# Last stage of an edge-gated graph layer: the add of the v part moves from GpSimd to VectorE, two tiles ahead, and gates and masks are handed on in halves

## Chip, cores and metric

The kernel runs on one core of a Trainium2 chip. The core has TensorE (PE, matrix products), VectorE (DVE), ScalarE (ACT), GpSimd (POOL) and SyncE (SP, which here only issues DMA), each with its own instruction queue that is worked off in order. On-chip memory is SBUF, with 128 partitions, and PSUM, eight banks into which TensorE writes. Engines wait for each other by semaphores. The metric is the device time of one execution in microseconds, lower is better.

## What is computed

```python
B, C, D = (16, 128, 256)            # x is 16 x 1024 x 256, adj 1024 x 1024
pre_u = einsum('bud,dk->buk', h_t, W1[:d])
pre_v = einsum('bvd,dk->bvk', h_t, W1[d:])
hidden = relu(pre_u[:, :, None, :] + pre_v[:, None, :, :] + b1)
S = sigmoid(einsum('buvk,ko->buvo', hidden, W2)[..., 0] + b2[0])
a_t = einsum('buv,bud->bvd', S * A_a, h_t)
m_t = einsum('uv,bud->bvd', A_m, h_t) * h_t
z_t = beta1 * h_t + beta2 * (einsum('bvd,de->bve', a_t, Wa) + ba) + beta3 * (einsum('bvd,de->bve', m_t, Wm) + bm)
```

Both A_a and A_m are adj, about 6% of whose entries are not zero. Only at those entries is S needed.

## The kernel before

Everything is float32. Earlier stages compute, per node, h_t Wa (`hWa_dram`) and all of z_t that does not depend on S (`base_dram`); then, for the entries (u, v) of adj that are not zero, a number per batch (`sum_dram`, 1024 x 1024 x 16). What is left of the gate's argument is a part of u and a part of v. The last stage, from line 1400 on, puts the gate together, masks it with adj and multiplies.

It goes over 8 v tiles (`vt`) of 128 nodes, and in each over 8 u tiles (`t`), 64 steps `k = 8 vt + t` in all. One step takes these passes over a 128 (u) x 128 (v) x 16 (batch) block of 1 MiB:

- SyncE loads the block into `raw` (2 buffers) in the order u, v, batch, and 64 KiB of adj into `adj_b` (5 buffers). Three larger loads stand in the same queue: `hWa_all`, 2 MiB for each u tile during the first v tile; `of_v`, 1 MiB for each v tile, one buffer, issued when all adds of the v tile before have read it; and `z`, 2 MiB for each v tile, one buffer, at t = 4, when the finished z of the v tile before has been stored.
- The add (L1457): `masked = raw + of_v`, written in the order u, batch, v. `masked` has 4 buffers, and `step_done(k - 4)` waits until TensorE has read the one to be written.
- The gates (L1513): ScalarE, 16 activations, one for each batch, in place, with the u part as bias.
- The mask (L1475): VectorE multiplies the gates by adj, in place.
- The product (L1493): TensorE, for each batch, `masked` (128 x 128) by `hWa_all` (128 x 256), summed over the eight t into one half of a PSUM bank. All eight banks are in use. In the trace a batch shows as 2 MATMUL instructions, a step as 32.
- `finish(vt)` (L1466): VectorE adds the eight banks to `z`, one after the other. It stands at t = 1 of the next v tile. TensorE may write a bank for the next v tile when it has been added. ScalarE issues the store of z (L1505) behind the gates of t = 3.

The names in what follows: "add t=5" is the add of the step t=5 of a v tile, "raw t=5" its load.

Of the kernel before, what the change touches and what calls it, by code (L numbers as in the profile page):

```python
# [5 lines left out]
def gnn_edges_kernel(nc, x, adj, W1, b1, W2, b2, Wa, ba, Wm, bm, beta1, beta2, beta3, out):  # L6
# [15 lines left out]
    ALU = mybir.AluOpType  # L22
# [3 lines left out]
    B, N, D = x.shape  # L26
# [39 lines left out]
    with ctx:  # L66
# [1332 lines left out]
        with ExitStack() as phase:  # L1399
            RAW, GM, ADJ = 2, 4, 5  # L1400
# [29 lines left out]
            with nc.Block() as block:  # L1430
                @block.sync
                def _(sp):
                    for vt in range(NT):
                        for t in range(NT):
                            k = vt * NT + t
                            if t == 0 and vt:
                                sp.wait_ge(raw_added, k)
                                load_of_v(sp, vt)
                            waits(sp, raw_added, k - RAW + 1)
                            sp.dma_start(raw[k % RAW][:], sum_uv[t * P:(t + 1) * P, vt * P:(vt + 1) * P, :]).then_inc(raw_loaded[k % RAW], 16)  # L1440
                            waits(sp, gate_masked, k - ADJ + 1)
                            sp.dma_start(adj_b[k % ADJ][:], adj[t * P:(t + 1) * P, vt * P:(vt + 1) * P]).then_inc(adj_loaded[k % ADJ], 16)
# [5 lines left out]

                @block.gpsimd
                def _(pool):  # L1450
                    for vt in range(NT):
                        pool.wait_ge(of_v_loaded, 16 * (vt + 1))
                        for t in range(NT):
                            k = vt * NT + t
                            pool.wait_ge(raw_loaded[k % RAW], 16 * (k // RAW + 1))
                            step_done(pool, k - GM)
                            nc.gpsimd.tensor_tensor(masked[k % GM][:].rearrange("p b v -> p v b"), raw[k % RAW][:], of_v[:], ALU.add).then_inc(raw_added, 1)  # L1457

                @block.vector
                def _(dve):  # L1460
# [8 lines left out]
                    nc.vector.tensor_scalar(of_u[:], of_u[:], half_sign[:, 0:1], betas[:, 3:4], ALU.mult, ALU.add).then_inc(u_ready, 1)  # L1469
                    for vt in range(NT):  # L1470
                        for t in range(NT):
                            k = vt * NT + t
                            dve.wait_ge(adj_loaded[k % ADJ], 16 * (k // ADJ + 1))
                            dve.wait_ge(gate_made, k + 1)  # L1474
                            nc.vector.tensor_tensor(masked[k % GM][:], masked[k % GM][:],  # L1475
                                                    adj_b[k % ADJ][:].rearrange("p (a v) -> p a v", a=1).broadcast_to([P, B, P]),
                                                    ALU.mult).then_inc(gate_masked, 1)
                            if t == 1 and vt:
                                finish(vt - 1)
                    finish(NT - 1)  # L1480
# [66 lines left out]
```

## Time and profile before

| | us |
|---|---|
| median of 3 runs | 3941.08 (3937.64 to 3946.14) |
| profiled execution | 3951.05, of it span 3949.3 |
| last stage, from 3368 to 3949 | 581 |
| TensorE busy in it | 474.0 |
| ScalarE busy in it | 400.3 |
| GpSimd busy in it | 330.8 |
| VectorE busy in it | 258.8 |

The span is the time from the first to the last instruction or transfer of one profiled execution. Busy time is the sum over the instructions of an engine, without its waits. TensorE's clock is granted in two levels, 1.2 and 2.4 GHz; its mean in the last stage is 0.91 of the full level.

### The profile page before, as it was taken

To read this page: it belongs to the slowest core of one execution; us is meant where nothing else is said; L and a number is where in the kernel's file an instruction comes from. 1 tells how busy PE (TensorE), PEld (TensorE's weight loads), DVE (VectorE), ACT (ScalarE), POOL (GpSimd) and SP (SyncE) were. 2 spreads that over 40 slices of the span, in tenths; PEclk is the share of its full clock that TensorE was granted. 3 is DMA by queue.
4 is the path that set the end of the run, shared out by engine and by line. 5 is a ranking of instruction groups with operands and counts; after the bars stand their busy time and mean duration, and the time that the engine had idled before them with its cause. 6 is when DMAs were issued, how large, how long until landed. Compare 5 with 4: busy or idle time off the path is not lost. (4 is left out here: it accounts for less than half of the span.)

```text
span 3949.3 us, 56078 instructions
## 1 busy us (share of the span) xinstructions
PE 3452.5 (87%) x14232; PEld 2670.5 (68%) x14232; DVE 2832.8 (72%) x4788; ACT 2318.1 (59%) x14050; POOL 1859.7 (47%) x2338
## 2 busy tenths in 40 slices
PE   4977877887877949999999999999999999578898
PEld 2655555555555637887888888888888887567677
DVE  4455555555555358999999999999999999354534
ACT  0111111111111127998999999999999998577765
POOL 2222222212112125666666666666666665465664
PEclk9989988998988979999999999999999999789999
DMA  4545544555465577566765666765766653956564
GB/s 147 187 168 199 208 171 168 184 209 180 175 217 189 194 178 161 140 172 150 170 157 141 150 137 166 169 168 133 185 145 163 158 128 71 316 203 228 185 214 164
DMA packets 342892, 685.83 MB, mean 174 GB/s; under 512 B 38782, under 2 KB 252648, under 8 KB 319720
## 3 DMA queue, kind: packets, MB, share of 16 engines
q1 hardware_dynamic: 304544, 612.07, 53.6%
q0 software_dynamic: 21504, 53.31, 4.4%
q10 hardware_dynamic: 16512, 16.78, 1.3%
q8 instruction: 116, 1.90, 0.2%
q14 instruction: 216, 1.77, 0.2%
HBM read 444.01 MB, written 256.18 MB: 177 GB/s over the span
## 5 line engine op out<-in xcount | busy, mean ns | idle before, releaser
L1169 ACT ACTIVATE junk<-psum_a 128x128 f32<-128x128 f32 x6144 | 1605.3, 296 | 238.3 <-PE psum_a L1073 172.3
L1169 ACT ACTIVATION_READ_ACCUMULATOR junk<-psum_a 128x1 f32 x6144 | 1381.8, 227 | 0.0
L1114 DVE TENSOR_REDUCE group_sum<-psum_d 128x56 f32<-128x896 f32 x1024 | 1111.2, 1085 | 84.7 <-PE psum_d L1073 44.6
L1072 PE MATMUL psum_d<-u_t,pk 128*128 128x512 f32 x2560 | 1006.5, 393 | 62.2 <-DMA v_t<-rows_dram 33.0
L1073 PE MATMUL psum_d<-v_t,pk 128*128 128x512 f32 x2560 | 999.9, 391 | 0.0
L1218 POOL DMA_INDIRECT sum_dram<-total,idx_all x512 | 505.8, 988 | 228.0 <-POOL total L1229 124.1
L1072 PEld LDWEIGHTS psum_d<-u_t,pk 128*128 128x128 f32 x2560 | 482.2, 188 | 186.0 <-issue 50.2
L1072 PE MATMUL psum_a<-u_t,pk 128*128 128x512 f32 x1536 | 605.6, 394 | 0.0
L1073 PE MATMUL psum_a<-v_t,pk 128*128 128x512 f32 x1536 | 599.3, 390 | 0.0
L1493 PE MATMUL z_psum<-hWa_all,masked 128*128 128x256 f32 x2048 | 474.0, 396 | 118.1 <-DVE masked L1475 71.3
L849 POOL TENSOR_TENSOR own<-whole 128x256 f32<-128x256 f32 x128 | 92.4, 722 | 998.6 <-issue 729.4
L1073 PEld LDWEIGHTS psum_d<-v_t,pk 128*128 128x128 f32 x2560 | 482.6, 189 | 98.4
L1493 PEld LDWEIGHTS z_psum<-hWa_all,masked 128*128 128x128 f32 x2048 | 407.2, 200 | 184.9 <-DVE masked L1475 74.5
L603 PE MATMUL wide<-adj_sb,h 128*128 128x512 f32 x1024 | 511.6, 622 | 0.0
L1513 ACT ACTIVATE masked<-masked,of_u,half_sign 128x128 f32<-128x128 f32 x1024 | 399.0, 480 | 151.7 <-POOL masked L1457 151.7
L673 ACT COPY hWa<-ring 128x512 f32<-128x512 f32 x64 | 37.5, 586 | 715.4 <-PE ring L625 715.4
L1475 DVE TENSOR_TENSOR masked<-masked,adj_b 128x2048 f32<-128x2048 f32 x64 | 220.3, 3445 | 307.8 <-ACT masked L1513 307.8
L1457 POOL TENSOR_TENSOR masked<-raw,of_v 128x2048 f32<-128x2048 f32 x64 | 330.9, 5186 | 230.0 <-DMA raw<-sum_dram 169.2
L1211 POOL TENSOR_TENSOR fold<-group_sum,group_sign 128x256 f32<-128x256 f32 x256 | 189.7, 741 | 394.6 <-DVE group_sum L1141 392.8
L587 PE MATMUL ring<-W_k,hT 128*128 128x258 f32 x1024 | 277.6, 431 | 108.9 <-ACT whole L666 107.5
L1111 DVE TENSOR_REDUCE late_sum<-psum_d 128x4 f32<-128x512 f32 x512 | 347.0, 678 | 0.4 <-PE psum_d L1073 0.4
L1072 PEld LDWEIGHTS psum_a<-u_t,pk 128*128 128x128 f32 x1536 | 289.0, 188 | 77.6 <-ACT junk L1169 20.5
(207 smaller groups left out, 4039.7 us busy)
## 6 DMA issues: line engine op xcount, KB each, us to landing
u_t<-rows_dram SPq DMA_DIRECT2D x126, 1024.0 KB
rows_dram<-split SPq DMA_DIRECT2D x128, 512.0 KB, 3.3
sum_dram<-zero SPq DMA_DIRECT2D x128, 512.0 KB, 5.0
pk<-pick_dram SPq DMA_DIRECT2D x512, 128.0 KB, 2.7
raw<-sum_dram SPq DMA_DIRECT2D x64, 1024.0 KB, 7.0
v_t<-rows_dram SPq DMA_DIRECT2D x36, 1024.0 KB, 13.1
whole_dram<-whole SPq DMA_DIRECT2D x128, 256.0 KB, 3.8
pick_dram<-pick SPq DMA_DIRECT2D x128, 256.0 KB, 2.0
```

Of the source, the lines that this page charges most:

```text
L587: last = nc.tensor.matmul(ring[:, w * BANK:w * BANK + CW], hT[:, c, t * P:(t + 1) * P], W1_k[:, c, w, :], start=(c == 0), stop=(c == DT - 1))
L603: last = nc.tensor.matmul(wide[:, c * N + n * BANK:c * N + (n + 1) * BANK], h[b % 2][:, t, c * P:(c + 1) * P], adj_sb[:, t, n * BANK:(n + ...
L1072: nc.tensor.matmul(dst, pk[n % PKS][:, at:at + P], part(u_t[k % 2][:], b, LB), start=True, stop=False)
L1073: return nc.tensor.matmul(dst, pk[n % PKS][:, SLOTS + at:SLOTS + at + P], part(v_t[n % VG][:], b, LB), start=False, stop=True)
L1111: return nc.vector.tensor_reduce(out_, in_, AX, ALU.add, apply_absolute_value=True)
L1114: nc.vector.tensor_reduce(out_[:, :, 1:EG], in_[:, :, GW:LATE].rearrange("p b (g k) -> p b g k", k=GW), AX, ALU.add, apply_absolute_value= ...
L1169: last = nc.scalar.activation(junk[:, a % RING_A, k * LATE:(k + 1) * LATE], psum_a[a % RING_A][:, k * LATE:(k + 1) * LATE], ACT.Abs, accum ...
L1218: nc.gpsimd.indirect_dma_start(out=sum_dram[:, :], out_offset=bass.IndirectOffsetOnAxis(ap=at, axis=0), in_=sums, in_offset=None, bounds_c ...
L1457: nc.gpsimd.tensor_tensor(masked[k % GM][:].rearrange("p b v -> p v b"), raw[k % RAW][:], of_v[:], ALU.add).then_inc(raw_added, 1)
L1475: nc.vector.tensor_tensor(masked[k % GM][:], masked[k % GM][:], adj_b[k % ADJ][:].rearrange("p (a v) -> p a v", a=1).broadcast_to([P, B, P ...
L1493: last = nc.tensor.matmul(z_psum[b // 2][:, (b % 2) * D:(b % 2 + 1) * D], masked[k % GM][:, b, :], hWa_all[:, t, b, :], start=(t == 0 and ...
L1513: last = nc.scalar.activation(masked[k % GM][:, b, :], masked[k % GM][:, b, :], ACT.Sigmoid, bias=of_u[:, t, b:b + 1], scale=half_sign[:, ...
```

## The change

The add goes from GpSimd, which has nothing left to do in this stage, to VectorE, with the same operands and the same output order. In VectorE's queue the adds of the steps 0 and 1 come first, then in each step k the add of step k+2 ahead of the mask of step k. At t = 1 `finish` stands ahead of the add and the mask, where it stood behind the mask. The gates are handed to VectorE after 8 and 16 batches, the mask is done in two instructions of 8 batches, and TensorE waits for each half. SyncE issues `adj_b` ahead of `raw`, no longer behind it.

```diff
-            RAW, GM, ADJ = 2, 4, 5
+            RAW, GM, ADJ, MASKS = 2, 4, 5, 2
...
+                            waits(sp, gate_masked, MASKS * (k - ADJ + 1))
+                            sp.dma_start(adj_b[k % ADJ][:], adj[t * P:(t + 1) * P, vt * P:(vt + 1) * P]).then_inc(adj_loaded[k % ADJ], 16)
                             waits(sp, raw_added, k - RAW + 1)
                             sp.dma_start(raw[k % RAW][:], sum_uv[t * P:(t + 1) * P, vt * P:(vt + 1) * P, :]).then_inc(raw_loaded[k % RAW], 16)
-                            waits(sp, gate_masked, k - ADJ + 1)
-                            sp.dma_start(adj_b[k % ADJ][:], adj[t * P:(t + 1) * P, vt * P:(vt + 1) * P]).then_inc(adj_loaded[k % ADJ], 16)
...
-                @block.gpsimd
-                def _(pool):
-                    for vt in range(NT):
-                        pool.wait_ge(of_v_loaded, 16 * (vt + 1))
-                        for t in range(NT):
-                            k = vt * NT + t
-                            pool.wait_ge(raw_loaded[k % RAW], 16 * (k // RAW + 1))
-                            step_done(pool, k - GM)
-                            nc.gpsimd.tensor_tensor(masked[k % GM][:].rearrange("p b v -> p v b"), raw[k % RAW][:], of_v[:], ALU.add).then_inc(raw_added, 1)
...
+                    def add_of_v(k):
+                        if k % NT == 0:
+                            dve.wait_ge(of_v_loaded, 16 * (k // NT + 1))
+                        dve.wait_ge(raw_loaded[k % RAW], 16 * (k // RAW + 1))
+                        step_done(dve, k - GM)
+                        nc.vector.tensor_tensor(masked[k % GM][:].rearrange("p b v -> p v b"), raw[k % RAW][:], of_v[:], ALU.add).then_inc(raw_added, 1)
+
+                    HB = B // MASKS
+                    for k in range(2):
+                        add_of_v(k)
                     for vt in range(NT):
                         for t in range(NT):
                             k = vt * NT + t
-                            dve.wait_ge(adj_loaded[k % ADJ], 16 * (k // ADJ + 1))
-                            dve.wait_ge(gate_made, k + 1)
-                            nc.vector.tensor_tensor(masked[k % GM][:], masked[k % GM][:],
-                                                    adj_b[k % ADJ][:].rearrange("p (a v) -> p a v", a=1).broadcast_to([P, B, P]),
-                                                    ALU.mult).then_inc(gate_masked, 1)
                             if t == 1 and vt:
                                 finish(vt - 1)
+                            if k + 2 < NT * NT:
+                                add_of_v(k + 2)
+                            dve.wait_ge(adj_loaded[k % ADJ], 16 * (k // ADJ + 1))
+                            for m in range(MASKS):
+                                rows_ = masked[k % GM][:, m * HB:(m + 1) * HB, :]
+                                dve.wait_ge(gate_made, MASKS * k + m + 1)
+                                nc.vector.tensor_tensor(rows_, rows_,
+                                                        adj_b[k % ADJ][:].rearrange("p (a v) -> p a v", a=1).broadcast_to([P, HB, P]),
+                                                        ALU.mult).then_inc(gate_masked, 1)
...
-                            pe.wait_ge(gate_masked, k + 1)
                             for b in range(B):
+                                if b % (B // MASKS) == 0:
+                                    pe.wait_ge(gate_masked, MASKS * k + b * MASKS // B + 1)
...
-                            last.then_inc(gate_made, 1)
+                                if (b + 1) % (B // MASKS) == 0:
+                                    last.then_inc(gate_made, 1)
```

What this does to VectorE's queue is seen at the turn from the first to the second v tile. Before, VectorE's rows from the mask of t=4 of the first v tile to the first add to z are (masked1 and adj_b0 are buffers; the brackets name the semaphores that a row waits for):

```order
L1475 TENSOR_TENSOR masked0<-masked0,adj_b4 128x2048 [waits gate_made,adj_loaded4]
L1475 TENSOR_TENSOR masked1<-masked1,adj_b0 128x2048 [waits gate_made,adj_loaded0]
L1475 TENSOR_TENSOR masked2<-masked2,adj_b1 128x2048 [waits gate_made,adj_loaded1]
L1475 TENSOR_TENSOR masked3<-masked3,adj_b2 128x2048 [waits gate_made,adj_loaded2]
L1475 TENSOR_TENSOR masked0<-masked0,adj_b3 128x2048 [waits gate_made,adj_loaded3]
L1475 TENSOR_TENSOR masked1<-masked1,adj_b4 128x2048 [waits gate_made,adj_loaded4]
L1466 TENSOR_TENSOR z<-z,z_psum0 128x512 [waits z_summed,z_loaded]
```

After the change, from the second half of the mask of t=4 to the mask of t=7, the add into masked0 that waits for of_v being that of t=0 of the second v tile:

```order
L1481 TENSOR_TENSOR masked0<-masked0,adj_b4 128x1024 [waits gate_made]
L1465 TENSOR_TENSOR masked3<-raw1,of_v 128x128x16 [waits gate_used,raw_loaded1]
L1481 TENSOR_TENSOR masked1<-masked1,adj_b0 128x1024 [waits gate_made,adj_loaded0]
L1481 TENSOR_TENSOR masked1<-masked1,adj_b0 128x1024 [waits gate_made]
L1465 TENSOR_TENSOR masked0<-raw0,of_v 128x128x16 [waits gate_used,raw_loaded0,of_v_loaded]
L1481 TENSOR_TENSOR masked2<-masked2,adj_b1 128x1024 [waits gate_made,adj_loaded1]
L1481 TENSOR_TENSOR masked2<-masked2,adj_b1 128x1024 [waits gate_made]
L1465 TENSOR_TENSOR masked1<-raw1,of_v 128x128x16 [waits gate_used,raw_loaded1]
L1481 TENSOR_TENSOR masked3<-masked3,adj_b2 128x1024 [waits gate_made,adj_loaded2]
```

The add that waits for `of_v` and its `raw` now stands ahead of the mask of t=6 (masked2) in the same queue.

SyncE's queue before, from the load of z at t=4 of the second v tile to the first two raw loads of the third (raw0 and raw1 are the two buffers):

```order
L1447 DMA z<-base_dram 128x16x256 [waits z_stored]
L1440 DMA raw1<-sum_dram 128x2048 [waits raw_added]
L1442 DMA adj_b3<-in_adj_dram 128x128 [waits gate_masked]
L1440 DMA raw0<-sum_dram 128x2048 [waits raw_added]
L1442 DMA adj_b4<-in_adj_dram 128x128 [waits gate_masked]
L1440 DMA raw1<-sum_dram 128x2048 [waits raw_added]
L1442 DMA adj_b0<-in_adj_dram 128x128 [waits gate_masked]
L987 DMA of_v<-linear_dram 128x2048 [waits raw_added]
L1440 DMA raw0<-sum_dram 128x2048 [waits raw_added]
L1442 DMA adj_b1<-in_adj_dram 128x128 [waits gate_masked]
```

The same place after the change:

```order
L1447 DMA z<-base_dram 128x16x256 [waits z_stored]
L1440 DMA adj_b3<-in_adj_dram 128x128 [waits gate_masked]
L1442 DMA raw1<-sum_dram 128x2048 [waits raw_added]
L1440 DMA adj_b4<-in_adj_dram 128x128 [waits gate_masked]
L1442 DMA raw0<-sum_dram 128x2048 [waits raw_added]
L1440 DMA adj_b0<-in_adj_dram 128x128 [waits gate_masked]
L1442 DMA raw1<-sum_dram 128x2048 [waits raw_added]
L987 DMA of_v<-linear_dram 128x2048 [waits raw_added]
L1440 DMA adj_b1<-in_adj_dram 128x128 [waits gate_masked]
L1442 DMA raw0<-sum_dram 128x2048 [waits raw_added]
```

Each raw load has moved behind the adjacency load of its step; the loads of z and of_v stand where they stood.

## Rows read from the trace of the kernel before

**Rows 1.** The page's first line.
```profile
span 3949.3 us, 56078 instructions
```

**Rows 2.** The last stage: length, busy us of each engine (instructions), clock, DMA share, GB/s.
```profile
3368.00:3949.00 581.00, 474.00 (x2048) 407.20 (x2048) 258.76 (x128) 400.26 (x1025) 330.84 (x64) 0.91 0.63 220
```

**Rows 3.** Waits of the last stage: who for whom, total us, times, longest us.
```profile
DVE masked L1475 <- ACT masked L1513: 307.8, 55, 14.4
POOL masked L1457 <- DMA raw<-sum_dram: 169.2, 30, 13.1
ACT masked L1513 <- POOL masked L1457: 151.7, 44, 8.6
...
PE z_psum L1493 <- DVE masked L1475: 71.3, 11, 36.2
...
PE z_psum L1493 <- DVE z L1466: 46.8, 7, 15.3
```

**Rows 4.** Timeline of a v tile: start us, us, engine, line, what, count.
```profile
3603.98 4.86 DVE L1466 TENSOR_TENSOR z<-z,z_psum 128x512 f32<-128x512 f32 x8
...
3604.80 36.23 PE L1493 MATMUL z_psum<-hWa_all,masked 128*128 128x256 f32 x160 [3.08 <-DVE z L1466]
3608.51 2.04 ACT L1513 ACTIVATE masked<-masked,of_u,half_sign 128x128 f32<-128x128 f32 x5 [0.29 <-POOL masked L1457]
...
3610.19 0.38 ACTq L1505 DMA_DIRECT2D out_dram<-z  x1
...
3617.72 0.37 SPq L1447 DMA_DIRECT2D z<-base_dram  x1
...
3620.87 0.43 SPq L1442 DMA_DIRECT2D adj_b<-in_adj_dram  x1
...
3628.36 9.06 POOL L1457 TENSOR_TENSOR masked<-raw,of_v 128x2048 f32<-128x2048 f32 x2 [10.25 <-DMA raw<-sum_dram]
...
3642.97 0.32 SPq L987 DMA_DIRECT2D of_v<-linear_dram  x1
...
3645.14 22.67 PE L1493 MATMUL z_psum<-hWa_all,masked 128*128 128x256 f32 x96 [4.11 <-DVE masked L1475]
...
3650.72 24.25 POOL L1457 TENSOR_TENSOR masked<-raw,of_v 128x2048 f32<-128x2048 f32 x4 [7.79 <-DMA raw<-sum_dram]
...
3671.29 36.46 PE L1493 MATMUL z_psum<-hWa_all,masked 128*128 128x256 f32 x160 [3.48 <-DVE z L1466]
```

**Rows 5.** TensorE in stretches of 4 us: busy us (instructions), granted clock, DMA share, GB/s.
```profile
3604.80:3608.80 4.00, 4.00 (x12) 0.63 0.39 152
3608.80:3612.80 4.00, 4.00 (x20) 1.00 0.41 140
```

**Rows 6.** Single lines: duration in ns, least/median/most, first and last start.
```profile
L1457 POOL TENSOR_TENSOR masked<-raw,of_v x64: 4528/4556/6631, 3368.0 to 3911.2; 128x2048 f32<-128x2048 f32 x64
...
L1475 DVE TENSOR_TENSOR masked<-masked,adj_b x64: 2275/2302/5798, 3380.2 to 3924.6; 128x2048 f32<-128x2048 f32 x64
...
L857 POOL TENSOR_TENSOR base<-base,bias_row x16: 4492/4496/6583, 97.3 to 1353.9; 128x2048 f32<-128x2048 f32 x16
...
L809 DVE TENSOR_TENSOR rank<-rank,row_start x8: 1224/1224/1227, 170.1 to 1144.1; 128x1024 f32<-128x1024 f32 x8
...
L777 DVE COPY counts<-rank x8: 176/4282/4294, 99.6 to 1026.3; 128x16 f32<-128x16 f32 x8
...
L815 DVE COPY lcount<-over_scan x8: 153/153/154, 175.7 to 1149.7; 128x1 f32<-128x1 f32 x8
...
L813 DVE TENSOR_SCALAR over<-rank x8: 693/694/696, 172.6 to 1146.7; 128x1024 f32<-128x1024 f32 x8
```

**Rows 7.** Timeline of the first v tile's end.
```profile
3435.01 23.67 PE L1493 MATMUL z_psum<-hWa_all,masked 128*128 128x256 f32 x96 [9.38 <-DVE masked L1475]
...
3436.98 4.55 POOL L1457 TENSOR_TENSOR masked<-raw,of_v 128x2048 f32<-128x2048 f32 x1 [4.26 <-DMA raw<-sum_dram]
```

**Rows 8.** Timeline of the last v tile.
```profile
3917.94 22.67 PE L1493 MATMUL z_psum<-hWa_all,masked 128*128 128x256 f32 x96 [4.05 <-DVE masked L1475]
```

## Prediction

> **What bounds the kernel now.** I read the span first [rows 1], then the stretch in which the changed code runs [rows 2]. It lasts 581 of 3949.3 us, and everything before it is untouched. In it TensorE is busy 474.0 us, ScalarE 400.3, GpSimd 330.8, VectorE 258.8: TensorE leads, but idles 107 us. The waits of the stretch come next [rows 3]: TensorE waits for VectorE's masks (71.3 us) and for its adds to z (46.8 us), VectorE for ScalarE's gates (307.8 us), ScalarE for GpSimd (151.7 us), and GpSimd for the loads of raw (169.2 us). So the chain runs load, add, gate, mask, matmul, and the loads pace it at two places of every v tile. Both are seen in the timeline [rows 4], where t counts the u tiles of a v tile from 0 to 7.
>
> First place, the store. At 3608.51 ScalarE starts the gates of t=3. The store of z is triggered at 3610.19, SyncE may issue the load of z only at 3617.72, when the store has landed, and raw of t=5 stands behind that load: GpSimd can add it at 3628.36. That is 19.85 us from the end of add t=3 (the gates follow it at once) to the start of add t=5. Second place, of_v. SyncE reloads the only of_v buffer at 3642.97, once add t=7 is done, and add t=0 of the next v tile starts at 3650.72: 7.75 us. Today only GpSimd stands still there; VectorE goes on masking tiles that are already gated, so TensorE's two pauses per v tile are short. The period is 3671.29 less 3604.80, 66.5 us.
>
> TensorE's own pace comes from the same rows: 160 instructions in 36.23 us and 96 in 22.67, both begun after a pause, so 64 take 13.56, a u tile (32) takes 6.8 us, and the first one after a pause 22.67 less 2 x 6.8, 9.1 us. The reason is in [rows 5]: in the 4 us from 3604.80, straight after an idle time, the granted clock averages 0.63 of 2.4 GHz (so most of it at 1.2), and 12 instructions show; in the next 4 us it is 1.00 and 20 show.
>
> **The change, part by part.** *Removed:* 64 adds on GpSimd, median 4556 ns [rows 6]. They also slowed the masks: the mask has a minimum of 2275 ns and a maximum of 5798 [rows 6], and VectorE's busy time of 258.8 [rows 2] less the adds to z, 8 x 4.86 [rows 4], is over 3.4 us a mask. That is freed time on an engine that waited 307.8 us anyway, and I book no gain for it by itself.
>
> *Halved masks:* 128x1024 of two SBUF operands takes 1224 ns on VectorE [rows 6], so a tile costs 2.45 us in place of 2.30, and TensorE may begin 1.2 us after the mask starts. Gates in halves cost ScalarE nothing: the same 16 activations, one more semaphore.
>
> *Added to VectorE:* 64 adds whose output steps 512 bytes from element to element (16 batches inside, 128 v outside), inputs contiguous. No row of VectorE shows such a write of this size. Bounds from the nearest rows: below, its contiguous 128x2048 multiply, 2.3 us; above, GpSimd's run of this very add, 4.53 us. GpSimd's rows don't tell whether the step costs anything: its contiguous add of that size takes 4496 ns and the stepping one 4556 [rows 6]. Two small VectorE rows do: the copy of 16 elements that lie 256 bytes apart takes 176 ns, the copy of one element 153, so 23 ns for 15 elements, 1.53 ns each; two-operand contiguous work costs (2302 - 1224)/1024 = 1.05. If stepping costs the add what lies between these two, 0.5, its element takes 1.53 ns and the add 3.2 us. But a contiguous one-operand instruction runs at (694 - 153)/1023 = 0.53 ns [rows 6]; if the copy would have done so too, stepping cost it 1.0, and the add would take 2048 x 2.05, 4.2 us. I take **3.6 us**, between these two, also near the middle of the outer bounds. The Trainium skill (Vector Engine (DVE) Microarchitecture Reference, section 5.2, Measured stream behaviour on trn2) says that a port keeps its full rate only in runs of at least two adjacent words, and lists 1.71 ns per column for an output hopping 4 KiB at each element, 2.50 for steps of 24 words. No row here shows either; by its 1.71 the add would be an estimated 3.58 us and the result below the same within 1 us, by 2.50 an estimated 5.2 us and some 4045 us in all.
>
> *Moved in the queues:* the adjacency load now stands ahead of raw on SyncE. It has long been free to go, but takes 0.43 us of issue [rows 4], so raw t=5 and raw t=0 each come 0.4 us later where they are issued right behind z and of_v.
>
> *The new waits, which decide.* add k+2 stands ahead of mask k in VectorE's queue. A wait of the add for its raw, for of_v or for TensorE to free a buffer (tile k-2 done) now also holds mask k, and with it TensorE. What was GpSimd's wait becomes everybody's.
>
> **One v tile after the change**, followed on VectorE from the end of add t=3, a being the price of an add:
> 1. Gates of t=3, store, load of z, raw t=5: 19.85 + 0.4 = 20.3 us. Only mask 1, add t=4 and mask 2 (8.5 us) lie beside it; VectorE stands 11.8 us.
> 2. add 5, mask 3, add 6, mask 4, add 7: 3a + 4.9. add 7 needs TensorE done with t=3, which starts 1.25 us after the end of add 5 and, after its pause, takes 9.1: 10.35 against 4.9 + a, a wait of 5.45 - a.
> 3. of_v and raw t=0: 7.75 + 0.4, say 8.1. Beside it lies mask 5 alone (2.45).
> 4. add 0, mask 6, add 1, mask 7, the same wait of 5.45 - a for t=6, add 2, mask 0, the 8 adds to z (4.86 us [rows 4]), add 3: 4a + 7.35 + 4.86 + the wait.
>
> Sum: 20.3 + 4.9 + 8.1 + 7.35 + 4.86 = 45.5, with the rest 45.5 + 7a + 2(5.45 - a) = 56.4 + 5a. At 3.6: **74.4 us against 66.5**.
>
> First v tile: loads arrive back to back and set it as before, so add 7 starts at 3437.0 as now [rows 7]. It ends at 3440.6, add 0 of the next tile runs 3448.7 to 3452.3, mask 6 frees TensorE at 3453.55, t=6 takes 9.1 and t=7 6.8: done 3469.45, where today it is 3458.7 [rows 7]. From there to the end of add 3 another 7.7 us (add 2 at 3462.65, mask 0, the adds to z, add 3 to 3477.16).
> Last v tile: no of_v behind it: 7.7 + 20.3 + 3.6 + 1.25 + 9.1 + 4 x 6.8 = 69.15.
> End: TensorE done at 3469.45 + 6 x 74.4 + 69.15 = 3985.0. Today the tail from TensorE's end at 3940.6 [rows 8] to the span's end is 8.7 us and it stays: span 3993.7, 44.4 above 3949.3. The profiled execution took 3951.05 where the runs have a median of 3941.08, so it lies 10 us above them, and I add the difference to the median: **3985.5 us**, 1.1% slower.
>
> **Rivals.**
> A, *the stepping write is free* (2.3 us, the contiguous row). Then TensorE doesn't pause before t=6 and the second wait is 0.85: period 45.5 + 16.1 + 3.15 + 0.85 = 65.6. First tile done 3466.85, last 65.25: 3925.7, span 3934.4, 14.9 less: 3926 us, faster. It decides below an add of about 2.65 us. For it: nothing else on VectorE is slow. Against: the 1.53 ns row. 0.13.
> Between, an add of 2.5 to 2.8 us: within 0.2%. 0.07.
> B, *the write costs as on GpSimd or more* (4.53): waits 0.92, period 79.05, first tile done 3471.3, last 72.0: 4017.6, span 4026.3, 77 more: 4018 us. 0.07.
> C, *two tiles ahead hides the loads*, and TensorE is the bound: 8 x 6.8 + 2.3 = 56.7 a period, 7 x 9.8 = 69 less: 3872 us. Against it: raw has two buffers, and [rows 4] show raw t=5 held by the store, not by an add. 0.03.
> My forecast, adds of 2.8 to 4.4 us, has 0.70.
>
> **Numbers.** About 0.2% (8 us) is what a measurement of this kernel can tell from no change. Within the forecast the prices 3.2 and 4.2 give about 3967 and 4007 (A and B lie 46 us an us of add below it and 35 above); the store and load times may be off by 1 us each in 7 periods. The upper end takes in B at 4018. Downwards I go to 3938, which holds the in-between case and leaves out A and C, 0.16. Faster: A, C and a third of the between, 0.18; same 0.05; slower 0.77.
>
> **What the changed profile would show.** The add on VectorE near 3.6 us (below 2.65 the sign turns); masks of 1.22 us with hardly any spread; two VectorE waits per v tile for raw, some 12 and 5.5 us, in place of GpSimd's; TensorE idle some 10 us before t=3 and 3 before t=6, with the lower clock after each; period near 74 us; no TensorE pause at a v tile's start beyond the first add to z. Wrong it is if TensorE runs on through t=3 (then the gates or the store come earlier than I think), or if raw t=5 is added sooner than 20 us after add t=3.

## The result, and the profile after

The changed kernel takes 3993.81 us (median of 4 runs, 3988.0 to 3995.45), the kernel before 3939.36 on the same chip (4 runs, 3934.83 to 3946.14): a ratio of 1.0134, interval 1.0116 to 1.0153. It is slower by 1.3%, some 54 us. The range of the prediction (3938 to 4018) holds the time, which lies 8.3 us above the 3985.5 forecast. The profiled span is 3991.4 us, where [rows 1] had 3949.3 and the forecast said 3993.7. The stage itself grew by more than the 42.1 us between the spans: its first VectorE instruction (L1459, L1469 before) starts at 3362.79 us where it started at 3365.52, since the unchanged stages ahead of it happened to end 2.7 us sooner. From there to the end of the span it is 628.6 us in place of 583.8, 44.8 more.

First the last stage as a whole, as in [rows 2] but in a window that begins 8 us sooner, and under it the costliest group of TensorE and the add on the page of the changed kernel:

```profile
3360.00:3992.00 632.00, 482.01 (x2048) 409.67 (x2048) 414.47 (x257) 399.74 (x1025) 0.00 (x0) 0.88 0.58 205
```

```profile
L1498 PE MATMUL z_psum<-hWa_all,masked 128*128 128x256 f32 x2048 | 482.0, 399 | 155.2 <-DVE masked L1481 155.2
...
L1465 DVE TENSOR_TENSOR masked<-raw,of_v 128x2048 f32<-128x2048 f32 x64 | 237.5, 3711 | 194.0 <-DMA raw<-sum_dram 156.8
```

VectorE is busy 414.5 us, ScalarE 399.7, TensorE 482.0. No engine's work alone has become the bound: TensorE still works longest and now waits 155 us, where it waited 118 (71.3 for masks and 46.8 for the adds to z, [rows 3]). Its busy time grew by 8 us (474.0 before), and from 3368 us on, as in [rows 2], its mean granted clock is 0.89 in place of 0.91. The waits, which answer to [rows 3]:

```profile
ACT masked L1518 <- DVE masked L1465: 196.7, 39, 11.7
DVE masked L1465 <- DMA raw<-sum_dram: 156.8, 21, 12.5
PE z_psum L1498 <- DVE masked L1481: 155.2, 25, 42.8
...
DVE masked L1465 <- PE z_psum L1498: 30.8, 14, 3.4
...
DVE z L1456 <- PE z_psum L1498: 11.3, 7, 10.3
DVE masked L1465 <- issue: 6.3, 1, 6.3
```

Before, VectorE waited 307.8 us for gates and GpSimd 169.2 us for raw. Now VectorE is the engine that waits for raw, 156.8 us, and TensorE waits 155.2 us for its masks. That the two are nearly equal means nothing: 42.8 of the 155.2 are the one wait at the start of the stage (36.2 before). What counts is the growth of TensorE's waits, 37 us, which with the 8 us of longer work makes the 45 us of the stage. ("issue" as a releaser is a wait for which the trace names none; the one of 6.3 us stands before add t=0 of the second v tile, where other v tiles wait for raw.) One v tile, answering to [rows 4]:

```profile
3620.99 3.71 DVE L1465 TENSOR_TENSOR masked<-raw,of_v 128x2048 f32<-128x2048 f32 x1
...
3624.73 2.03 ACT L1518 ACTIVATE masked<-masked,of_u,half_sign 128x128 f32<-128x128 f32 x5 [4.17 <-DVE masked L1465]
3625.80 14.08 PE L1498 MATMUL z_psum<-hWa_all,masked 128*128 128x256 f32 x64 [1.62 <-DVE masked L1481]
3626.40 0.38 ACTq L1510 DMA_DIRECT2D out_dram<-z  x1
...
3633.93 0.37 SPq L1447 DMA_DIRECT2D z<-base_dram  x1
3634.35 2.03 SPq L1440 DMA_DIRECT2D adj_b<-in_adj_dram  x1
3636.42 0.43 SPq L1442 DMA_DIRECT2D raw<-sum_dram  x1
...
3645.01 3.63 DVE L1465 TENSOR_TENSOR masked<-raw,of_v 128x2048 f32<-128x2048 f32 x1 [12.28 <-DMA raw<-sum_dram]
...
3649.75 22.43 PE L1498 MATMUL z_psum<-hWa_all,masked 128*128 128x256 f32 x96 [9.87 <-DVE masked L1481]
...
3658.48 3.73 DVE L1465 TENSOR_TENSOR masked<-raw,of_v 128x2048 f32<-128x2048 f32 x1 [1.82 <-PE z_psum L1498]
...
3662.24 0.32 SPq L987 DMA_DIRECT2D of_v<-linear_dram  x1
...
3670.02 3.70 DVE L1465 TENSOR_TENSOR masked<-raw,of_v 128x2048 f32<-128x2048 f32 x1 [5.63 <-DMA raw<-sum_dram]
...
3674.83 21.14 PE L1498 MATMUL z_psum<-hWa_all,masked 128*128 128x256 f32 x96 [2.64 <-DVE masked L1481]
...
3682.11 3.79 DVE L1465 TENSOR_TENSOR masked<-raw,of_v 128x2048 f32<-128x2048 f32 x1 [0.35 <-PE z_psum L1498]
...
3688.00 4.86 DVE L1456 TENSOR_TENSOR z<-z,z_psum 128x512 f32<-128x512 f32 x8
...
3692.78 3.68 DVE L1465 TENSOR_TENSOR masked<-raw,of_v 128x2048 f32<-128x2048 f32 x1
```

Read down from the end of add t=3 at 3624.70. The store is triggered at 3626.40, has landed by 3633.93, when SyncE issues the load of z, and raw t=5, behind the loads of z and of the adjacency, is added at 3645.01. The mask of t=3 stands behind that add, so TensorE waits 9.87 us. The same happens at 3670.02 behind of_v, where the pause is 2.64 us.

### The profile page after: what moved, and what is told of

The parts are those of the page before. It is cut to its first block and busy times, and to the rows that moved or that the text cites. A ratio compares the mean times of both kernels' runs of the same rounds, so it can differ in the third digit from the quotient of the medians.

```text
span 3991.4 us, 56149 instructions
## 1 busy us (share of the span) xinstructions
PE 3459.8 (87%) x14232; PEld 2671.3 (67%) x14232; DVE 2988.5 (75%) x4916; ACT 2323.0 (58%) x14050; POOL 1533.0 (38%) x2274
## 5 line engine op out<-in xcount | busy, mean ns | idle before, releaser
L1498 PE MATMUL z_psum<-hWa_all,masked 128*128 128x256 f32 x2048 | 482.0, 399 | 155.2 <-DVE masked L1481 155.2
L1465 DVE TENSOR_TENSOR masked<-raw,of_v 128x2048 f32<-128x2048 f32 x64 | 237.5, 3711 | 194.0 <-DMA raw<-sum_dram 156.8
L1073 PEld LDWEIGHTS psum_a<-v_t,pk 128*128 128x128 f32 x1536 | 289.5, 188 | 57.0
```

The lines of the kernel that those rows point to most:

```text
L1073: return nc.tensor.matmul(dst, pk[n % PKS][:, SLOTS + at:SLOTS + at + P], part(v_t[n % VG][:], b, LB), start=False, stop=True)
L1465: nc.vector.tensor_tensor(masked[k % GM][:].rearrange("p b v -> p v b"), raw[k % RAW][:], of_v[:], ALU.add).then_inc(raw_added, 1)
L1498: last = nc.tensor.matmul(z_psum[b // 2][:, (b % 2) * D:(b % 2 + 1) * D], masked[k % GM][:, b, :], hWa_all[:, t, b, :], start=(t == 0 and ...
```

## The experiments

Each median stands beside that of the kernel before on the same chip. The ratio is taken round by round, so it need not be that of the two medians. The runs were made on different chips, on which the kernel before has medians from 3939.4 to 3947.2, so a difference between the medians of two rows is good to some 5 us.

| Run | us | range | before | ratio, interval |
|---|---|---|---|---|
| the change | 3993.8 | 3988.0–3995.5 | 3939.4 | 1.0134, 1.0116–1.0153 |
| e1 contiguous add | 3940.4 | 3936.3–3945.6 | 3943.8 | 0.9994, 0.9984–1.0003 |
| e2 mask first | 3960.9 | 3956.0–3964.9 | 3943.8 | 1.0048, 1.0031–1.0064 |
| e3 add on GpSimd | 3934.7 | 3930.8–3936.9 | 3943.8 | 0.9974, 0.9963–0.9984 |
| e4 z load late | 3930.2 | 3923.9–3934.0 | 3943.8 | 0.9962, 0.9948–0.9976 |
| e5 before, z load late | 3940.0 | 3936.1–3943.4 | 3945.0 | 0.9990, 0.9980–0.9999 |
| e6 = e3, z load late | 3875.9 | 3872.9–3879.6 | 3945.0 | 0.9828, 0.9811–0.9844 |
| e7 = e2, z load late | 3907.9 | 3907.4–3918.2 | 3945.0 | 0.9918, 0.9901–0.9935 |
| e8 of_v once | 3963.0 | 3960.3–3966.9 | 3945.0 | 1.0053, 1.0036–1.0070 |
| e9 = e5, finish first | 3885.6 | 3884.3–3888.5 | 3945.6 | 0.9847, 0.9832–0.9862 |
| e10 = e6, finish last | 3934.3 | 3929.5–3940.0 | 3945.6 | 0.9966, 0.9952–0.9980 |
| e11 adjacency behind raw | 3977.7 | 3976.0–3980.1 | 3945.6 | 1.0080, 1.0066–1.0094 |
| e12 = e6, adjacency behind raw | 3869.9 | 3867.8–3870.8 | 3947.2 | 0.9806, 0.9792–0.9819 |

**e1, the add without its step.** How much of the loss is the price of the write? The add here writes its numbers in the order v, batch, so the gates and masks meet them in the wrong places; only the time counts.

```diff
-nc.vector.tensor_tensor(masked[k % GM][:].rearrange("p b v -> p v b"), raw[k % RAW][:], of_v[:], ALU.add)
+nc.vector.tensor_tensor(masked[k % GM][:].rearrange("p b v -> p (b v)"), raw[k % RAW][:].rearrange("p v b -> p (v b)"), of_v[:].rearrange("p v b -> p (v b)"), ALU.add)
```

> The changed kernel with one edit: VectorE's add writes masked one element after another, in the order of raw (v, batch), and no longer in the order batch, v, so the gates see the numbers in another order. Same instructions, same waits. My theory prices a v tile at 56.4 + 5a with a the add: at 2.3 us for the contiguous add it gives 65.6 us a v tile and about 3926 us in all, some 60 us below the changed kernel and slightly below the kernel before. Rival 'the stepping write costs nothing, the waits in the queue are all': add stays at 3.7 us or the time stays within 10 us of the changed kernel.

The single line of the add and the waits:

```profile
L1465 DVE TENSOR_TENSOR masked<-raw,of_v x64: 2284/2292/2294, 3370.2 to 3903.6; 128x2048 f32<-128x2048 f32 x64
```

```profile
DVE masked L1465 <- DMA raw<-sum_dram: 174.2, 21, 14.0
...
PE z_psum L1498 <- DVE masked L1481: 112.8, 15, 42.0
```

The add takes 2.29 us, and the time falls to 3940.4, 53 us under the change by the medians and 1.4% by the ratios. The period (from one start of TensorE at t=3 to the next) is (3894.32 - 3498.12)/6 = 66.0 us, where rival A said 65.6. So A's arithmetic was right and its condition wrong. The step costs 3.715 - 2.292 = 1.42 us an add. VectorE still waits for raw, 174 us in place of 157, and 41 us for TensorE in place of 31: of the 91 us that the 64 adds save, these waits take 27. So even with a contiguous write the kernel is no faster than before. It doesn't reach the 3926 expected of it: the span of its profiled run, 3939.8, is 5.4 above rival A's 3934.4, and the rest is the 10 us carried from before's profiled run to its median, of which more below.

**e2, the mask ahead of the add.** All else as in the change.

```diff
-                            if k + 2 < NT * NT:
-                                add_of_v(k + 2)
                             dve.wait_ge(adj_loaded[k % ADJ], 16 * (k // ADJ + 1))
...
                                                         ALU.mult).then_inc(gate_masked, 1)
+                            if k + 2 < NT * NT:
+                                add_of_v(k + 2)
```

> The changed kernel with one edit: in VectorE's queue the two halves of mask k stand ahead of add k+2, not behind it. Same work on every engine. Theory 'what an add waits for (store chain, of_v) holds the mask behind it': mask k gets out before the wait, TensorE has one tile more to do during it, a v tile falls from 74.4 to about 71 us and the time by 25 to 35 us, to some 3960 to 3970. Rival 'VectorE simply has too much work': no change within 8 us, since the work is the same.

It takes 3960.9: 33 us less than the change, with the same adds at the same price (median 3729 ns) on the same engine. Only the order of the queue differs, so the coupling is shown. The v tile is 69.7 us long in the mean. Its waits:

```profile
DVE masked L1465 <- DMA raw<-sum_dram: 118.0, 15, 12.5
...
PE z_psum L1498 <- DVE masked L1479: 91.3, 16, 34.9
...
DVE masked L1465 <- issue: 41.0, 7, 6.4
PE z_psum L1498 <- DVE z L1456: 26.6, 7, 4.0
```

VectorE waits for its loads nearly as long as in the change. The row for raw is 38.8 us shorter, but the waits before add t=0, 5.5 to 6.4 us each, now stand under "issue": 118.0 + 41.0 = 159.0 us against 156.8 + 6.3 = 163.1. What is gone are the waits of the adds for TensorE, 30.8 us in the change and none here: TensorE gets each mask ahead of the wait, is further on, and has freed the buffer when the add asks for it. The two differences make 34.9 us, about the 33 that the kernel gains. From the second v tile up to its last add VectorE never stands but for loads, so what is left of the 69.7 us is its own work and 18.2 us for them. In the timeline of a v tile:

```profile
3672.09 29.55 PE L1498 MATMUL z_psum<-hWa_all,masked 128*128 128x256 f32 x128 [4.00 <-DVE z L1456]
...
3702.30 3.64 DVE L1465 TENSOR_TENSOR masked<-raw,of_v 128x2048 f32<-128x2048 f32 x1 [12.24 <-DMA raw<-sum_dram]
...
3707.05 13.15 PE L1498 MATMUL z_psum<-hWa_all,masked 128*128 128x256 f32 x51 [5.41 <-DVE masked L1479]
```

The add waits 12.24 us for raw as before, but the mask of t=3 is done ahead of it. TensorE gets four u tiles (128 instructions) before it stops, and the pause is 5.41 us in place of 9.87. (The view ends at 3720, and cuts the last row short.)

**e3, the add back on GpSimd,** halves and the order of the loads kept.

```diff
+                @block.gpsimd
+                def _(pool):
...
+                            nc.gpsimd.tensor_tensor(masked[k % GM][:].rearrange("p b v -> p v b"), raw[k % RAW][:], of_v[:], ALU.add).then_inc(raw_added, 1)
...
-                            if k + 2 < NT * NT:
-                                add_of_v(k + 2)
```

> The changed kernel with the add back on GpSimd, as in the kernel before; halves of gates and masks, finish ahead of the mask and the adjacency load ahead of raw stay. Theory 'the move of the add is the whole loss': within 8 us of the kernel before (3931 to 3947), since the two load chains pace GpSimd as before and TensorE starts at most a little earlier. Rival 'halves, the place of finish or the adjacency load ahead of raw cost': it stays 10 us or more above the kernel before.

3934.7, ratio 0.9974: the halves, the place of finish and the adjacency load together bring 0.26%. The move of the add (with its place in the queue) is the whole loss.

**e4, the load of z later** (behind the raw load of t=6, not t=4), to take the store out of the way of raw.

```diff
-                            if t == 4:
+                            if t == 6:
```

> The changed kernel with one edit: SyncE issues the load of z at t = 6 of a v tile, behind raw t=6, and not at t = 4. Theory 'raw t=5 is late because it stands behind the load of z, which waits for the store': the 12 us wait of VectorE before add t=5 goes; the wait moves to raw t=7 and is partly covered; a v tile falls from 74.4 to about 63 us, the time by some 70 to 85 us, to about 3910 to 3925. Rival 'the bandwidth or the two raw buffers set it': VectorE waits as long at another add and the time falls by under 15 us.

```profile
PE z_psum L1498 <- DVE masked L1481: 103.9, 26, 45.3
DVE masked L1465 <- DMA raw<-sum_dram: 69.2, 16, 8.7
...
DVE masked L1465 <- issue: 35.1, 6, 6.3
```

63.5 us less than the change. The wait for raw falls to 69.2 us, and six waits before add t=0, 35.1 us, stand under "issue" again, so with them it falls from 163.1 to 104.3. The store's wait in SyncE's queue is thus worth more than the 54 us of the whole loss. That is no contradiction: e1, e2, e4 and e8 give back 53, 33, 63.5 and 31 us, together far more than 54, because each shortens the same chain of waits through VectorE's queue, so the loss can't be shared out among them. The time lies 5 us above the range that was expected, the period at (3868.48 - 3543.66)/5 = 65.0 us where 63 was. What is left is of_v and the step's price.

**e5, the same in the kernel before** (t=7).

```diff
-                            if t == 4:
+                            if t == 7:
```

> The kernel before with one edit: the load of z is issued at t = 7, not at t = 4. The theory that the store-then-load chain holds raw t=5 in the kernel before too, but is partly covered there since only GpSimd waits: the 10 us wait of GpSimd before add t=5 goes and the time falls by 20 to 35 us, clearly less than the 63.5 us that the same edit gave the changed kernel. Rival 'the chain cost the kernel before just as much': it falls by 55 us or more.

A miss: 5 us gained, not 20 to 35, and the interval nearly reaches no change. Its waits, and TensorE at the start of a v tile:

```profile
POOL masked L1457 <- PE z_psum L1493: 138.2, 34, 12.9
POOL masked L1457 <- DMA raw<-sum_dram: 90.6, 21, 13.1
...
PE z_psum L1493 <- DVE z L1466: 73.9, 7, 19.8
```

```profile
3668.42 58.12 PE L1493 MATMUL z_psum<-hWa_all,masked 128*128 128x256 f32 x256 [9.03 <-DVE z L1466]
```

GpSimd's wait for raw did fall, from 169.2 to 90.6 us, but its wait for TensorE to free a buffer rose from 53.2 to 138.2. TensorE ran a whole v tile (256 instructions) without a pause. But then it stood 9 us for the adds to z. These stand behind the mask of t=1 in VectorE's queue, which waits for the gates of t=1, for its add, for add t=0 and for of_v. So the pause had only moved. From this came e9 and e10, which move nothing but the adds to z.

**e6, e3 with the load of z at t=7.** The edits are those of e3 and e5.

> Add on GpSimd, gates and masks in halves, finish ahead of the mask, adjacency ahead of raw, and the load of z at t = 7. Here GpSimd's own waits hold nobody's mask and the store chain is gone; TensorE should be near its own pace, 57 to 61 us a v tile, and the time 50 to 80 us below the kernel before, 3865 to 3895. If GpSimd's adds, slowed by VectorE's masks, are the next bound: 62 us or more a v tile and 3905 or more.

3875.9: where the adds to z stand ahead of the mask, as they do in the changed code, the late load brings 59 us (3934.7 to 3875.9). Alone in the kernel before it brought 5.

**e7, e2 with the load of z at t=6.**

> The changed kernel with both edits: mask k ahead of add k+2, and the load of z at t = 6. If the two waits are separate costs the gains add: 33 us (mask first) and 63 us (z late) from the changed kernel, about 3900 or some less, since the mask-first order had its gain mostly at the store chain: 3900 to 3920. Rival 'both edits repair the same wait': no lower than the late load alone, 3925 to 3932.

3907.9. e2 took 33 us off the change, e4 63.5, together they take 86: nearly a sum, so the coupling in VectorE's queue and the store's wait in SyncE's are two causes.

**e8, of_v loaded once.**

```diff
-                            if t == 0 and vt:
-                                sp.wait_ge(raw_added, k)
-                                load_of_v(sp, vt)
...
-                        if k % NT == 0:
-                            dve.wait_ge(of_v_loaded, 16 * (k // NT + 1))
+                        if k == 0:
+                            dve.wait_ge(of_v_loaded, 16)
```

> The changed kernel with of_v loaded once, at the start, and kept for all v tiles: the seven later loads of of_v are left out, so all v tiles but the first use the wrong v part. My step 3 says that this load makes VectorE wait 5.6 us at each turn of a v tile; without it raw t=0 has 7 us from its release and mostly covers itself: a v tile falls by 3 to 6 us with the pause of TensorE before t=6, and the time by 20 to 40 us, to 3955 to 3975. Rival 'the raw load alone would be as late': under 10 us.

3963.0, 31 us less than the change, 4.4 us for each of the seven v tiles that reload of_v. The pause before t=6 is gone: from t=3 on TensorE runs 192 instructions, up to t=0 of the next v tile, in one burst of 43.5 to 44.9 us.

**e9, e5 with finish ahead of the mask's waits.**

```diff
+                            if t == 1 and vt:
+                                finish(vt - 1)
                             dve.wait_ge(adj_loaded[k % ADJ], 16 * (k // ADJ + 1))
...
-                            if t == 1 and vt:
-                                finish(vt - 1)
```

> The kernel before, whole masks, with the load of z at t = 7 and finish ahead of the mask of t = 1. The late load alone gave 0.1%, since TensorE then waited 9 us at each turn of a v tile for the adds to z, which stood behind a mask that waited for of_v, add and gate. If finish ahead of that mask is what was missing, most of the 59 us come: 3885 to 3905. Rival 'the halves are what was missing': no lower than 3920.

```profile
3641.89 55.49 PE L1493 MATMUL z_psum<-hWa_all,masked 128*128 128x256 f32 x256 [2.76 <-DVE z L1466]
```

3885.6, a gain of 1.5% over the kernel before from two moved statements. The pause is 2.76 us in place of 9.03, and the 256 instructions take 55.49 us, not 58.12: in the 4 us from 3641.89 the granted clock is 1.00, in the 4 us from 3668.42 of e5 it was 0.50.

**e10, e6 with finish behind the masks,** the reverse of it.

> The best version so far (add on GpSimd, halves, z at t = 7) with finish put back behind the mask of t = 1. If the place of finish is what matters, TensorE again waits some 8 us at each turn and it rises from 3876 to 3920 or more. Rival 'the halves are what matters': it stays within 15 us of 3876.

```profile
3674.76 56.98 PE L1497 MATMUL z_psum<-hWa_all,masked 128*128 128x256 f32 x256 [7.91 <-DVE z L1466]
```

3934.3: 58 us of e6's gain are lost again. The place of finish is the cause of e5's miss, shown from both sides.

**e11, the adjacency load behind raw,** the rest as in the change.

```diff
-                            waits(sp, gate_masked, MASKS * (k - ADJ + 1))
-                            sp.dma_start(adj_b[k % ADJ][:], ...)
                             waits(sp, raw_added, k - RAW + 1)
                             sp.dma_start(raw[k % RAW][:], ...)
+                            waits(sp, gate_masked, MASKS * (k - ADJ + 1))
+                            sp.dma_start(adj_b[k % ADJ][:], ...)
```

> The changed kernel with the adjacency load behind raw again, as before the change. I booked 0.4 us for it at two places of a v tile, so the time falls by 3 to 6 us, at most 0.15%. Rival 'the issue of the adjacency load behind the load of z costs what its row shows, 1.7 to 2.0 us (a full ring)': 12 us or more less.

3977.7, 16 us less than the change by the medians and 0.54%, 21 us, by the ratios, where 3 to 6 were expected. So the rival's number came true, but not its reason: behind the load of z the move brings next to nothing. From the issue of the load of z to add t=5 it is 10.82 us (3626.66 to 3637.48) in place of 11.08 in the v tile shown, and 11.00 in place of 11.16 in the mean of seven; from of_v's issue to add t=0 7.13 (3655.20 to 3662.33) in place of 7.78, and 7.27 in place of 8.15 in the mean of six. In sum that is 1.0 us a v tile against the 0.8 of the prediction, or 7 us in seven. The period though falls by 2.7 us, from 74.4 to (3928.79 - 3498.79)/6 = 71.7. The rest is TensorE behind its pauses. The six bursts from t=3 on last 23.41 us in the mean in the changed kernel and 22.90 in e11, the six from t=6 on 22.37 and 21.13. With the loads' 1.0, by which the two pauses are shorter, that makes 1.0 + 0.51 + 1.24 = 2.75 us, the 2.7 of the period. The bursts from t=6 on of the changed kernel, two of them:

```profile
3527.13 24.11 PE L1498 MATMUL z_psum<-hWa_all,masked 128*128 128x256 f32 x96 [3.36 <-DVE masked L1481]
...
3603.05 21.13 PE L1498 MATMUL z_psum<-hWa_all,masked 128*128 128x256 f32 x96 [3.18 <-DVE masked L1481]
```

Of the six, two last 24.11 us (pauses 3.36 and 3.14), one 22.57 (3.01), and three 21.13 or 21.14 (3.18, 2.67, 2.64). TensorE's first 4 us and the next 4 of the first of these rows, then the first 4 of the second:

```profile
3527.13:3531.13 4.00, 4.00 (x9) 0.50 0.72 266
3531.13:3535.13 4.00, 4.00 (x15) 0.74 0.57 199
...
3603.05:3607.05 4.00, 4.00 (x19) 1.00 0.69 260
```

In e11 the same pause is 1.84 to 2.40 us long, and every one of these bursts takes 21.1:

```profile
3667.15 21.10 PE L1498 MATMUL z_psum<-hWa_all,masked 128*128 128x256 f32 x96 [2.05 <-DVE masked L1481]
```

A fall costs 1.4 or 3.0 us of TensorE's time. That the shorter pause of e11 is what keeps the clock up is argued, not shown: the two were run on different chips, and the length of a pause alone doesn't decide. In e9 five v tiles begin after pauses of 2.41 to 2.91 us and take 55.49, a sixth after 2.67 and takes 57.18. In e6, six v tiles of 256 instructions begin after a short pause: four after 1.53 to 1.75 us, which take 55.49, and two after 2.03 and 2.09, which take 1.7 us more:

```profile
3579.24 57.17 PE L1497 MATMUL z_psum<-hWa_all,masked 128*128 128x256 f32 x256 [2.03 <-DVE z L1466]
3638.01 55.49 PE L1497 MATMUL z_psum<-hWa_all,masked 128*128 128x256 f32 x256 [1.60 <-DVE z L1466]
```

What else decides stays open.

**e12, the best of it together:** e6 with the adjacency load behind raw.

> The best version (add on GpSimd, halves, finish ahead of the mask, z at t = 7) with the adjacency load behind raw. In the changed kernel the same edit gave 16 us, of which by the traces only 0.9 us a v tile are the loads and the rest the clock, which no longer falls in TensorE's pause before t = 6. Here TensorE pauses under 2.1 us a v tile and has no such pause to shorten: 0 to 8 us less, 3868 to 3877. Rival 'the adjacency load ahead of raw costs 2 us a v tile by itself': 14 us or more less.

3869.9, ratio 0.9806: 1.9% faster than before.

```profile
L1497 PE MATMUL z_psum<-hWa_all,masked 128*128 128x256 f32 x2048 | 451.5, 383 | 61.5 <-DVE masked L1480 39.2 <-DVE z L1466 22.3
```

TensorE is busy 451.5 us in place of 474.0 before, for the same 2048 instructions, and waits 61.5 us in place of 118. From 3519 to 3860 its mean granted clock is 1.00. The second v tile still begins after a pause of 15.00 us and takes 57.44; each of the six from the third on is 55.49 us of work behind a pause of 0.87 to 1.52, with no fall of the clock. The 56.7 us period that rival C gave TensorE as its floor is reached, with the add on GpSimd and loads that no longer hold TensorE, and not by two tiles of lead on VectorE.

## Why the prediction was right, step by step

**The added wait.** Right, and with the price of the add it is the cause: e2 lets the mask out ahead of it (33 us), e4 shortens it at its source (63.5 us), and e3, which takes the add off VectorE, takes away the whole loss. The forecast said VectorE waits of some 12 and 5.5 us per v tile for raw; in the v tile above they are 12.28 and 5.63.

**The price of the add.** Taken as 3.6 us from between 3.2 and 4.2, measured 3.715 (median). The two readings of VectorE's small rows, 3.2 and 4.2, bracketed it; GpSimd's rows (4556 against 4496 ns) would have said that the step is free. An element of the stepping write costs (3715 - 2292)/2048 = 0.69 ns more than one of the contiguous write, between the 0.5 and 1.0 ns of the two readings. These stood on thin ground, so part of the hit is luck: the 176 ns of the 16-element copy are the least of eight, whose median is 4282 ns [rows 6], and by the code (L777) that copy steps in what it reads, where the add steps in what it writes. By the Trainium skill (Vector Engine (DVE) Microarchitecture Reference, section 5.2) an output hopping 4 KiB takes 1.71 ns a column; the trace has 3715/2048 = 1.81 ns at a hop of 512 bytes, with the instruction's fixed cost in it. So the measured price lies near the hop's row and far from the 2.50 of the 24-word row. (For that row the prediction's estimate should read some 4041 us and not 4045; by its own steps an add of 3.2 us gives 3971 and not 3967, since the slope above 2.65 us is 35 us a microsecond and not 46.) e1 gives what it is worth: 53 us for 1.42 us an add, 37 us of kernel for each microsecond of add. The prediction had 46 below its value and 35 above.

**Masks.** Said 1.22 us with little spread: 1.21, none over 1.24. No gain was booked for this, and no run shows it by itself.

**The period, by the four steps** in the v tile shown. (1) From the end of add t=3 to add t=5: 3624.70 to 3645.01, 20.3 us, predicted 20.3. Its parts hold too: 1.70 us to the trigger of the store (1.68 before), 7.53 to the issue of the load of z (7.53), and from there 11.08 to the add in place of 10.64, the 0.4 of the adjacency load. (2) To the end of add t=7: 17.2 us, predicted 17.55, with a wait for TensorE of 1.82 where 1.85 was said. (3) To add t=0: 7.8, predicted 8.1. (4) To the end of the next add t=3: 3670.02 to 3696.46, 26.4 against 28.5. Of these 2.1 us the wait for t=6 is 1.5: it was 0.35 and not 1.85, because here TensorE kept its clock after the pause of 2.64 us (1.00 in the 4 us from 3674.83). The other 0.6 is three masks, which hold the queue 2.25 us a tile and not 2.45:

```profile
3498.50 2.33 DVE L1481 TENSOR_TENSOR masked<-masked,adj_b 128x1024 f32<-128x1024 f32 x2
...
3500.75 3.71 DVE L1465 TENSOR_TENSOR masked<-raw,of_v 128x2048 f32<-128x2048 f32 x1
```

The wait is the term that was mis-sized in this v tile, and it isn't the same in each: the six periods are 77.1, 72.9, 71.9, 75.4, 76.7 and 72.4 us. The long ones hold a 24.11 or 22.57 us burst, the short ones 21.1. Their windows:

```profile
3499.75:3576.82 77.07, 62.22 (x256) 0.88 0.51 184
...
3649.75:3721.62 71.87, 57.65 (x256) 0.93 0.54 197
```

256 instructions of the same kind take 62.2 us at a mean granted clock of 0.88 and 57.7 at 0.93. The mean of the six is 74.4 us, the predicted 74.4. That it agrees to a tenth is luck, since two errors cancel. VectorE's waits were forecast at 11.8 + 5.65 + 1.85 + 1.85 = 21.15 us and are 12.4 + 6.0 + 2.8 + 1.6 = 22.8 in the mean (for raw t=5, raw t=0, and TensorE's t=3 and t=6); its work was forecast at 53.3 us and is 51.6, since a mask holds the queue for 2.25 us and not 2.45. An add holds it for 3.6 us, as booked: the next row starts some 0.15 us before the 3.7 are over.

The 66.5 us against which the prediction set its 74.4 was one v tile of before. The six periods there have a mean of 67.3, with one of 73.4 among them (the others are 65.2 to 67.5), so the change costs 7.1 us a v tile and not 7.9.

**First and last v tile.** Start of t=6 in the first: predicted 3453.55, found

```profile
3451.22 22.78 PE L1498 MATMUL z_psum<-hWa_all,masked 128*128 128x256 f32 x96 [4.99 <-DVE masked L1481]
```

2.3 us sooner: its add t=7 starts at 3434.13, where GpSimd's started at 3436.98 [rows 7]. But the whole stage starts 2.7 us sooner here, and counted from its first instruction add t=7 comes after 71.3 us in place of 71.5, as the prediction took it. At the start of the later v tiles TensorE runs on from t=7 into t=0 (one burst of 96), as said. The forecast doesn't have the pause of 1.6 us that follows before t=1, whose mask stands behind the adds to z and add t=3; in the v tile shown no wait of VectorE, whose queue sets the period, hangs on it. TensorE ends near 3982.7, predicted 3985.0, and the span's end follows 8.7 us later as before (3991.4). So the 2.3 us that the span missed come from the stages ahead, which the change doesn't touch. The stage grew by 44.8 us, the forecast had 44.4.

**The median.** The forecast missed it by 8.3 us, more than the 2.3 of the span, and in the other direction. The step that failed is the last one: the profiled run of before lay 10 us above the median of its runs, and the forecast carried that over as if it belonged to the median of the changed kernel. The profiled run of the changed kernel took 3993.1, 0.7 below its median of 3993.8. The plain sum of the forecast span and the 1.75 us around it (3951.05 - 3949.3) would have given 3995.5. Most of the 10 us may be seen in the trace of before: the v tile of 73.4 us is 7 us longer than the mean of the others, because TensorE stood 15 us for the adds to z at its end:

```profile
3744.67 36.27 PE L1493 MATMUL z_psum<-hWa_all,masked 128*128 128x256 f32 x160 [15.28 <-DVE z L1466]
```

The changed kernel has no such wait. No trace of a run of before at its median is kept, so this stays argued. The same offset is in e1's miss.

**The moved adjacency load** was priced at 2 x 0.4 us a v tile, and the loads show 1.0, of it 0.16 behind z and 0.88 behind of_v, so the sum was right and its halves were not. Without it the kernel is 16 to 21 us faster and not 6, the rest being TensorE's time behind its pauses, which the price left out.

**Rivals.** A's time was right for a free step (e1), and its condition, an add under 2.65 us, was not met. B was off by the price. C's floor was reached, but only with the add back on GpSimd and the loads freed (e12). The prediction named both levers, the store's wait and of_v, as the bound of the kernel before, but gave no price for TensorE's wait for the adds to z [rows 3], 46.8 us. e5 shows it to be the next wait in line.

## What to carry to other kernels

An in-order queue turns every wait in it into a wait of all that stands behind it: an operation that waits for a load goes behind the results that are ready to be made, not ahead of them (33 us here). That an engine has time to spare, as VectorE had with 258.8 of 581 us busy, doesn't say that it can take a wait. When a wait is removed, move in the same step what becomes late next: the later load of z alone gave 5 us, and with the adds to z moved up 60. And a single profiled run's distance from its median is not to be carried into a forecast.

## What was not expected of the hardware

- A write that steps 512 bytes costs VectorE 3715 ns against 2292 for the contiguous one of the same size (e1), and GpSimd next to nothing (4556 ns against 4496 for another, contiguous add of that size, [rows 6]).
- After pauses of nearly the same length TensorE has its full clock or a fall that costs 1.4 to 3.0 us: 3.18, 2.67 and 2.64 us without and 3.36, 3.14 and 3.01 with one in the changed kernel, 1.84 to 2.40 without one in e11, 2.03 and 2.09 with one in e6, 2.41 to 2.91 without and 2.67 with one in e9. What decides is not shown.
- Whichever load SyncE issues right behind that of z takes long to issue: 1.31 to 2.03 us for the adjacency load in the seven later v tiles here, where 0.43 is common, and 1.46 to 2.17 for raw in the kernel before. Why is not shown.
- The store of z, which the code has behind the 16 gates of t=3, is triggered 1.7 us after the first of these activations starts (3624.73 and 3626.40), not after the last.
